# Scan: the last image's turned values stored in eight pieces, and gate's first values fetched later

## What is computed

```python
xz = x @ Win;  xb, z = jnp.split(xz, 2, axis=-1)          # 256 channels each
xb = silu(conv3x3_depthwise(xb) + conv_b)
xf = xb.reshape(Bb, Cd, L)                                 # pixels by rows
xt = transpose(xb).reshape(Bb, Cd, L)                      # pixels by columns
xs = stack([xf, xf[..., ::-1], xt, xt[..., ::-1]])         # four directions
x_dbl = einsum('bcl,cd->bdl', xs_flat, Wxproj)             # dt (8), B (1), C (1)
A = -jnp.exp(A_log)
# for every direction, image and channel, over 4096 pixels:
#   delta = softplus(dt_w @ dt + dbias);  h = exp(delta * A) * h + delta * u * B;  y = h * C + u * D
y  = y0 + y1 + y2 + y3                                     # turned back to rows
yz = y * silu(z);  yn = gamma * (yz - mean) / sqrt(var + 1e-05) + beta
out = yn @ Wout
```

## Time and profile before

| | us |
|---|---|
| median of 3 runs | 4366.94 |
| lowest and highest run | 4362.61, 4369.41 |
| the profiled execution | 4366.15 |
| its span, first to last instruction | 4364.4 |
| start of `convolve` (first load issued) | 3108.54 |
| start of `scan` (first load issued) | 3586.66 |
| DVE's first recurrence in `scan` | 3601.43 |
| end of the span | 4364.4 |

### The profile page before, as it was taken

The page is one execution under the profiler, slowest core; times in us unless marked ns, Lnnn a source line. Parts: engine busy times, 40 slices in busy tenths (PEclk is TensorE's granted clock), DMA queues, the critical chain, the costliest instruction groups (busy, mean ns, idle before and its releaser), DMA issues. The chain is left out here.

```text
span 4364.4 us, 73508 instructions
## 1 busy us (share of the span) xinstructions
PE 3960.9 (91%) x25466; PEld 3025.3 (69%) x25466; DVE 3165.2 (73%) x7667; ACT 2753.0 (63%) x6175; POOL 1220.4 (28%) x1284
## 2 busy tenths in 40 slices
PE   6888888699999999999999999978799976889899
PEld 4666666488988989889988899965566642333247
DVE  3666666577777777877778777758466658887775
ACT  3666666467777777777777676647534437776643
POOL 1444444200002000010001000015124448886763
PEclk9999999799999999999999999989899985878779
DMA  7777776200001000010001000031223344554446
GB/s 212 207 198 201 199 196 182 90 22 22 22 20 44 20 23 20 24 41 18 25 15 38 19 8 11 11 85 63 81 94 139 135 157 146 181 161 159 145 154 206
DMA packets 301372, 414.08 MB, mean 95 GB/s; under 512 B 37322, under 2 KB 162250, under 8 KB 299978
## 3 DMA queue, kind: packets, MB, share of 16 engines
q1 hardware_dynamic: 288714, 392.45, 29.3%
q0 software_dynamic: 12288, 16.92, 1.5%
HBM read 255.72 MB, written 150.99 MB: 93 GB/s over the span
## 5 line engine op out<-in xcount | busy, mean ns | idle before, releaser
L864 ACT ACTIVATE l_ph<-l_T 128x512 fp32r<-128x512 f32 x1024 | 611.7, 597 | 548.1 <-PE l_T L777 548.1
L974 DVE TENSOR_TENSOR l_pl<-l_T,l_ph 128x512 fp32r<-128x512 f32 x1024 | 706.9, 690 | 274.7 <-ACT l_ph L864 274.0
L963 DVE CUSTOM_DVE_ANT_0 l_pr<-l_S,l_zero 128x512 f32<-128x512 f32 x1024 | 704.5, 688 | 74.7 <-PE l_S L700 11.2
L869 ACT ACTIVATE l_pr<-l_pr,l_st 128x512 f32<-128x512 f32 x1024 | 731.6, 715 | 1.1 <-DVE l_st L969 1.0
L789 PE MATMUL l_O<-l_ph,l_vh 128*128 128x256 f32 x2048 | 661.8, 323 | 12.2 <-DVE l_pl L974 11.8
L777 PE MATMUL l_T<-l_ident,l_pr 128*128 128x128 f32 x4096 | 612.7, 272 | 0.0
L777 PEld LDWEIGHTS l_T<-l_ident,l_pr 128*128 128x128 f32 x4096 | 507.6, 140 | 136.2
L790 PE MATMUL l_O<-l_ph,l_vl 128*128 128x256 f32 x2048 | 577.9, 282 | 0.0
L791 PE MATMUL l_O<-l_pl,l_vh 128*128 128x256 f32 x2048 | 576.5, 281 | 0.0
L1005 POOL TENSOR_TENSOR l_xs<-l_xs,l_bob 128x128 f32<-128x128 f32 x128 | 57.3, 460 | 1643.7 <-DMA l_xs<-x 1642.6
L698 PE MATMUL l_S<-l_kh,l_qh 128*128 128x512 f32 x1024 | 417.4, 408 | 1.1 <-DVE l_st L963 1.0
(11 more groups left out here) (239 smaller groups left out, 8197.4 us busy)
## 6 DMA issues: line engine op xcount, KB each, us to landing
l3b_u<-ub SPq DMA_DIRECT2D x128, 512.0 KB, 3.9
hls<-l_hl SPq DMA_DIRECT2D x64, 512.0 KB, 4.7
l_qs<-hls SPq DMA_DIRECT2D x96, 256.0 KB, 3.9
l_ks<-hls SPq DMA_DIRECT2D x96, 256.0 KB, 4.0
l_xc<-x1t SPq DMA_DIRECT2D x64, 256.0 KB, 2.7
zs<-l_tmp SPq DMA_DIRECT2D x64, 256.0 KB, 2.2
ub<-l3a_u SPq DMA_DIRECT2D x32, 512.0 KB, 3.2
ub<-l_planes SPq DMA_DIRECT2D x8, 2048.0 KB, 10.9
```

The source lines that it names most:

```text
L864: e.activation(ph[:, i, :], psT[:, i, :], ACT.Copy).then_inc(p_hi, 1)
L869: e.activation(pr[:, s, es], pr[:, s, es], ACT.Exp, bias=st[:, s, 9:10], scale=SC, accum_out=st[:, s, 10 + k:11 + k]).then_inc(exped, 1)
L963: e.tensor_tensor_reduce(pr[:, s, ks], psS[:, bk, :], zero[:].broadcast_to([128, 512]), 1.0, -3.0e38, ALU.add, ALU.max, st[:, s, kc:kc + 1 ...
L974: e.tensor_tensor(pl[:, i, :], psT[:, i, :], f32(ph[:, i, :]), ALU.subtract).then_inc(p_lo, 1)
```

## The change

`store_turned(3)` no longer stands at the end of `convolve`. The scan has a `store_turned(i)` of its own, for i = 0 to 7: one transfer of 128 partitions x 1024 values (512 KB) each, issued by SP at T = 1, 4, 7, ..., 22 behind the loads of u. The three first fetches of z go from ahead of the loop to T = 26, 27 and 28. The counts awaited of `turned_out[1]` become 160 (2 + 8 transfers of 16). And the exponential and the sign of `cA` leave `layer2`: ACT does both in the scan, between its first six softplus and its first six decays, each awaited before the next.

```diff
@@ layer2
-            w.wait_ge(conv_weights, 208)
-            e.activation(cA, cA, ACT.Exp).then_inc(A_exped, 1)
...
-            w.wait_ge(A_exped, 1)
-            e.tensor_scalar(cA, cA, -1.0, None, ALU.mult).then_inc(weighed, 1)
@@ convolve
-            store_turned(NI - 1)
@@ scan
                 if n == 2:
-                    w.wait_ge(K.turned_out[1], 64)
+                    w.wait_ge(K.turned_out[1], 160)
...
+            def store_turned(i):
+
+                h, cs = i // 4, slice(1024 * (i % 4), 1024 * (i % 4) + 1024)
+                e.dma_start(ub[1, h, 3, :, cs], planes[:, 1, h, cs]).then_inc(K.turned_out[1], 16)
...
-            for j in range(3):
-                fetch(j)
             for T in times:
                 if T >= 0 and T % 2 == 0 and T // 2 + 4 < M // 2:
                     load(T // 2 + 4)
+                i, late = divmod(T - 1, 3)
+                if 0 <= i < 8 and not late:
+                    store_turned(i)
+                if T in (26, 27, 28):
+                    fetch(T - 26)
...
+                if b == 0:
+                    e.activation(cA, cA, ACT.Exp).then_inc(A_ready, 1)
+                    w.wait_ge(A_ready, 1)
+                    e.activation(cA, cA, ACT.Copy, scale=-1.0).then_inc(A_ready, 1)
+                    w.wait_ge(A_ready, 2)
...
                         if k == 1:
-                            w.wait_ge(K.turned_out[1], 64)
+                            w.wait_ge(K.turned_out[1], 160)
```

More of the change, by code:

```diff
@@ L1039, in layer2 @@
         X_full, G_full, A_full, R_full, O_full = (P.sem(n) for n in ("X_full", "G_full", "A_full", "R_full", "O_full"))
-        X_free, gated, rooted, normed, A_exped = P.sem("X_free"), P.sem("gated"), P.sem("rooted"), P.sem("normed"), P.sem("A_exped")
+        X_free, gated, rooted, normed = P.sem("X_free"), P.sem("gated"), P.sem("rooted"), P.sem("normed")
         prepared, rows, sums, scaled, left, added, stats, moments, spread, inv, shift = (
@@ L1646, in scan @@
         soft, decayed = P.sem("soft"), P.sem("decayed")
-        rooted, scaled = P.sem("rooted"), P.sem("scaled")
+        A_ready, rooted, scaled = P.sem("A_ready"), P.sem("rooted"), P.sem("scaled")
         zeroed, scanned, c_done, gated = (P.sem(x) for x in ("zeroed", "scanned", "c_done", "gated"))
```

## The result

The changed kernel takes 4354.06 us (median of 17 runs, 4347.55 to 4361.55) against 4363.56 us of the kernel before in the same session (17 runs, 4358.16 to 4370.31). The ratio is 0.9975, 95% interval 0.9967 to 0.9982: faster by 7.9 to 14.4 us, 10.9 in the middle (the two medians alone differ by 9.5). The profiled execution took 4348.17 us, its span 4346.4. Measured again in two later sessions the ratio was 0.9970 (0.9959 to 0.9982) and 0.9977 (0.9967 to 0.9986). One run of the kernel before, 11795 us at a granted clock of 0.305, is left out of these ratios.

A forecast was written before the change was run, and what follows sets the result against it. The scan's start was taken as bound by a load of u behind two stores: 6.8 us at the first recurrence plus 1.2 us from a shorter Wout wait, nothing elsewhere, 8.0 us, so 4359 us; range 4353.5 to 4364.5.

The forecast's parts named there:

- What bounds the start: Scan's start: first load of u waits behind two 2 MB stores; without them POOL's first du ends 9.6 us earlier.
- The landing of the first load: Scan's start: with the stores gone, the first load of u lands in 3.9 us, the median of later loads.
- The rival in which the four loads crowd each other: Scan's start: four loads of u land together, first recurrence at 3596.4, gain 6.7 us, 4360 us; chance 0.08.
- cA: Scan's start: two small ACT operations add 0.6 us before the first decay; first recurrence still 6.8 us earlier.
- The weights: Scan's start: Wout issued at 3598.1, DVE waits 0.4 us for it, unit 3 starts 8.0 us earlier.
- The pieces, z and layer2: Scan and end of layer2: pieces and z fetches cost nothing; stage barriers taken as nothing, 0.3 us at most together.
- that sign: Stage starts: convolve and the scan were to start where they did before, within 0.3 us.
- The fixed price that the Trainium skill gives a transfer: Scan's pieces: 2.0 us per transfer, 12 us more in all for eight; forecast as hidden by the loads' lead.
- a landing beyond the lead: Early scan: loads landing later than the lead of about 12 us would hold POOL, and DVE behind it.
- a shift of the first recurrences is a shift of the whole scan: Whole scan: recurrences follow without such a wait, so time gained at the first ones carries through.
- a sign of error that the 8 us might be gone at the end: Scan's end: forecast wrong if the 8 us are there at unit 32 and gone at the span's end.
- The term for the scan's body in the sum: Scan behind its start: nothing gained or lost there, so nothing added to the 8.0 us.

The follow-up runs named there:

- e1: Kernel before with the eight pieces in place of the two stores, cA and the z fetches left where they were; ratio 0.9983 to the kernel before.
- e3: Changed kernel with all eight pieces issued ahead of the scan's four first loads of u; ratio 0.9998 to the kernel before.
- e5: Changed kernel with cA computed at the end of layer2 as before; ratio 0.9975 to the kernel before.
- e4: Changed kernel with a second store of each piece right behind it, 8 MB in 16 transfers; ratio 0.9978 to the kernel before.

## Why the prediction was right and wrong

*What bounds the start.* Right. The first load of u lay behind the stores, and with them gone POOL's first du starts 8.0 us earlier; e1 shows that it is the stores, and e3 that the place in the queue is the cause.

*The landing of the first load.* Mis-sized: 3.9 us taken from later loads, 5.5 us measured with four loads together. It cost nothing, as ACT ends the wait now, with 1.1 us to spare. The rival in which the four loads crowd each other was right in kind and small in size.

*cA.* Right: 0.6 us taken, 0.48 measured (e5), ACT the releaser of the first recurrence. The first recurrence came 6.84 us earlier, forecast 6.8.

*The weights.* Right: Wout issued at 11.7 us, forecast 11.4, and landed in 2.2 us. The wait is 0.17 us, forecast 0.4; the 0.2 us saved went to the product with gamma, 0.87 us in place of 0.48. Unit 3 is 7.99 us earlier, forecast 8.0, and 7.7 us against the other three traces of before. The forecast was read from the trace with the longest wait for Wout, 1.71 us.

*The pieces, z and layer2.* Right: no wait for any of them, and e4 shows a factor of two in reserve; the end of `layer2` gave nothing. `convolve` did not start within 0.3 us of where it had, but 4.0 us earlier; its distance from the end of `layer2` was the same, so that sign told of scatter ahead of it and not of the change. The pieces land in 5.9 us. The fixed price that the Trainium skill gives a transfer ("DMA: Bandwidth & Descriptors", "Anatomy of one DMA", which is on the path of transfers that GpSimd issues, where these are SP's) never reached the path: a landing beyond the lead, its condition here, was never near, with 6.3 us in e4.

*The step that failed* is the sentence that a shift of the first recurrences is a shift of the whole scan. It holds from unit 3 to unit 32 to 0.1 us and not beyond, where PE is the bound in part and its clock changes level. I had named as a sign of error that the 8 us might be gone at the end; they were there and some 3 us more by the timed runs; in the traces 748.6 to 751.2 us from unit 3 to the end stand against 754.9 to 757.1. What ties that to the change stays open, as said above. The term for the scan's body in the sum, nothing, should have been a term of its own with a width of 3 us or more on both sides, worked out from the rows of that stretch: the pairs of 5.3 and 6.4 us stand in the trace of before as well.

*The chances.* I gave 0.58 to a change within 0.2% and 0.39 to faster. The forecast of 8.0 us stood 0.7 us under the line, so a body term with its width would have made the two about equal. That the range of times held the median is in part luck, since the baseline came down by 3.4 us. I took the scatter from the spread of three runs; the sessions here show more: medians of the kernel before in six sessions went from 4361.8 to 4367.7 us.

## What to carry to other kernels

A large store that nothing waits for soon is not free at the end of a stage: it stands ahead of the next stage's first loads in the queue, and 4 MB held up the first one's use by 8.0 us here. Put it behind them, in parts small enough to take turns with loads that have a lead; a lead of 12 us against a landing of 6 hid twice the traffic. Count the gain only to the next stretch where PE is the bound with a changing clock, and give that stretch a width of its own in the forecast. To attribute what is left, hold the start back by known amounts and time many runs; single traces of one kernel differed by 2.6 us in that stretch here, and of kernels with nearly the same start by 8.

## What the runs showed of the hardware that was not expected

SP's issues take longer when 4 MB are in the queue: four loads took 4.21 us to issue behind the two stores, eight pieces in a row 7.91 us in e3, and a load 0.32 us in a quiet queue. The two small products with gamma took 0.48 us together when DVE had waited for them and 1.14 us when it had not. Units 3 to 32 of the scan took the same time to 0.09 us (62.44 to 62.53) in 20 traces of eleven kernels, with the pieces beside them once, twice or not at all; behind unit 32, where the clock changes level, the same traces spread from 748.6 to 757.1 us to the end.
